# Scores from split fp32r pairs in the attention phase, and the experts' matmuls ahead of the next projection

## What is computed

```python
x = conv(inputs, conv_w) + conv_b             # 3 taps, 1024 -> 3*256, split into q, k, v
qh, kh, vh = (q @ wq + bq), (k @ wk + bk), (v @ wv + bv)   # 16 heads of 64, blocks of 128 tokens
scores = einsum('bqhe,bkhe->bhqk', qh / 8, kh) # causal inside each block of 128
o = softmax(scores) @ vh;  o = o @ wo + bo;  attn = o @ proj_w + proj_b
x = layernorm(x + attn)
base = x @ W_base.T + b_base
w = relu(softmax(x @ W_gate.T) - sigmoid(x @ W_thr.T + b_thr) / 8);  w = w / sum(w)
out = base + 2 * einsum('ner,ne,eor->no', x @ A, w, B)     # 8 experts of rank 16
x = layernorm(x + out)
```

## Time and profile before

| | |
|---|---|
| median of 3 runs | 1757.93 us (1756.76 to 1758.82) |
| the profiled execution | 1758.82 us, span of its instructions 1757.0 us |
| PE busy | 1702.0 us, 97% of the span |
| PEld busy | 1532.1 us, 87% |
| DVE busy | 1298.4 us, 74% |
| ACT busy | 678.1 us, 39% |
| POOL busy | 328.2 us, 19% |
| mean granted TensorE clock | 0.989 |

### The profile page before, as it was taken

One profiled execution on the slowest core, in us unless ns is written; L12 is line 12 of the kernel. 1 busy time (PEld: TensorE's weight loads), 2 busy tenths in 40 slices (PEclk: granted clock), 3 DMA queues, 4 the chain that ended last, 5 costly groups with the idle time before them and its releaser, 6 DMA issues. The chain is left out here.

```text
span 1757.0 us, 32959 instructions
## 1 busy us (share of the span) xinstructions
PE 1702.0 (97%) x11968; PEld 1532.1 (87%) x11968; DVE 1298.4 (74%) x3089; ACT 678.1 (39%) x1817; POOL 328.2 (19%) x272
## 2 busy tenths in 40 slices
PE   6899999999999899999999999989999999999998
PEld 5899999999999778888888888869999898999887
DVE  8977679987677566666666666777787887878785
ACT  4333324332333466766767766761111111111110
POOL 5200003400000100100101002053333333333331
PEclk9999999999999899999999999999999999999999
DMA  4323223332234200110110102141212111121211
GB/s 142 115 80 96 80 82 108 127 114 78 79 95 156 102 1 10 40 48 0 48 48 0 48 22 79 64 137 47 77 54 81 54 68 66 61 73 54 81 39 49
DMA packets 48805, 123.04 MB, mean 70 GB/s; under 512 B 5488, under 2 KB 13680, under 8 KB 48240
## 3 DMA queue, kind: packets, MB, share of 16 engines
q1 hardware_dynamic: 48752, 122.36, 21.2%
HBM read 88.79 MB, written 33.55 MB: 70 GB/s over the span
## 5 line engine op out<-in xcount | busy, mean ns | idle before, releaser
L388 PE MATMUL conv_acc<-x_split,weights 128*128 128x256 f32 x4608 | 557.8, 284 | 30.9 <-DVE weights L314 23.5
L388 PEld LDWEIGHTS conv_acc<-x_split,weights 128*128 128x128 f32 x4608 | 554.8, 191 | 33.6 <-DVE weights L314 25.2
L1315 PE MATMUL ps_f<-weights 128*128 128x266 f32 (+2 forms) x1728 | 329.5, 343 | 0.0
L1315 PEld LDWEIGHTS ps_f<-weights 128*128 128x128 f32 x1728 | 277.4, 189 | 23.9
L247 ACT ACTIVATE x_split<-x_mixed 128x1024 fp32r<-128x1024 f32 x128 | 135.7, 1060 | 308.2 <-PE conv_acc L388 278.7
L309 DVE TENSOR_TENSOR x_split<-x_mixed,x_split 128x1024 fp32r<-128x1024 f32 x128 | 158.7, 1240 | 100.5 <-ACT x_split L247 100.5
L803 DVE CUSTOM_DVE_ANT_0 scores_and_probs<-ps_scores,causal_mask 128x128 f32<-128x128 f32 x512 | 118.6, 287 | 127.6 <-PE ps_scores L923 123.8
L710 ACT ACTIVATE scores_and_probs<-scores_and_probs,score_neg_max 128x128 f32<-128x128 f32 x512 | 197.9, 391 | 4.8 <-DVE score_neg_max L808 4.7
L1151 ACT ACTIVATE gate_exp<-h_and_gate,gate_neg_max 128x8 f32<-128x8 f32 x32 | 9.6, 301 | 348.5 <-DVE gate_neg_max L1226 348.5
L676 POOL TENSOR_TENSOR weights<-conv_tile,weights 128x1024 fp32r<-128x1024 f32 x14 | 35.7, 2551 | 439.1 <-ACT weights L696 353.9
L1315 PE MATMUL ps_f<-late_weights,weights 128*128 128x266 f32 (+2 forms) x576 | 116.1, 337 | 0.0
(11 more groups left out here) (115 smaller groups left out, 2423.1 us busy)
## 6 DMA issues: line engine op xcount, KB each, us to landing
x_raw<-in_xT SPq DMA_DIRECT2D x128, 257.0 KB, 2.7
conv_tile<-in_x SPq DMA_DIRECT2D x32, 512.0 KB, 3.4
out<-out_tile SPq DMA_DIRECT2D x32, 512.0 KB, 2.7
convT_scratch<-features_out SPq DMA_DIRECT2D x16, 768.0 KB, 3.5
conv_tile<-convT_scratch SPq DMA_DIRECT2D x16, 768.0 KB, 6.3
conv_w_raw<-in_conv_w SPq DMA_DIRECT2D x16, 576.0 KB, 4.0
weight_stage<-in_ffn_w SPq DMA_DIRECT2D x8, 581.0 KB, 3.7
yT_scratch<-features_out SPq DMA_DIRECT2D x8, 512.0 KB, 3.7
```

The source lines that it names most:

```text
L388: last = nc.tensor.matmul(acc[f][k // 2][:, k % 2, :], w[:, c, a, k, f * P:(f + 1) * P], xs[:, c % XS, b, k, :], start=(c == 0 and k % 2 = ...
L1315: mm = nc.tensor.matmul(ps_f[par][n][:, 0:b0 - a0], x1T[:, par, a, kc, :], wf[kc][:, b, a0:b0], start=(kc == 0 and k == 0), stop=(n == 2 a ...
```

## The change

**First part (attention).** q and k are stored as fp32r pairs, high and low. ScalarE writes the high parts: q in one instruction, k in two (`k_out`, one for each head of the pair, because each head's k goes to columns of its own). VectorE gets a new step `qk_out` of three instructions that write the low parts, straight from PSUM: two for k (64 partitions each) and one for q. It stands between `normalize` and `mask_max`. `q_ready` and `k_ready` are now raised by VectorE. k has for each block two groups of 128 columns, one for each head: head 0's k in partitions 0 to 63 of the first group, head 1's in partitions 64 to 127 of the second; the other halves are zero, written once by four memsets on GpSimd. So one matmul of 128 x 128 weights (both heads of q) and 256 columns gives the scores of both heads for one block. `make_scores` makes three of them (`PASSES`) for each block, 12 in all, in place of 8 plain fp32 ones. Bank 0 now holds blocks 0 and 1 and bank 1 blocks 2 and 3, and `s_done` is raised after blocks 1 and 3. The two late feed-forward weights lie in the same memory as q and k from the last phase on.

**Second part (feed-forward).** `experts(i)` stands ahead of `project(i + 2)`.

```diff
-        qk = sb("q_and_k", [P, 2, 2, ST], F32)
-        self.k, self.q = qk[:, 0, :, :], qk[:, 1, :, :]
-        late = sb("late_weights", [P, self.LATE * 2 * WCOLS], F32R)
+        k_cols, q_cols = 2 * 2 * BLK * 2 * P, 2 * 2 * ST
+        pair = sb("q_k_pairs", [P, k_cols + q_cols], F32R)
+        self.k = pair[:, 0:k_cols].rearrange("p (i h b j n) -> p i h b j n", i=2, h=2, b=BLK, j=2)
+        self.q = pair[:, k_cols:].rearrange("p (i h n) -> p i h n", i=2, h=2)
...
+            for i in range(2):
+                for j in range(2):
+                    nc.gpsimd.memset(k[rows(1 - j), i, :, :, j, :].bitcast(F32), 0.0).then_inc(k_zeroed, 1)
+            pool.wait_ge(k_zeroed, 4)
...
-                nc.scalar.activation(q[:, s % 2, :], ps_qt[:], ACT.Identity, bias=bq[:, s:s + 1]).then_inc(q_ready, 1)
+                nc.scalar.activation(q[:, s % 2, HI, :], ps_qt[:], ACT.Identity, bias=bq[:, s:s + 1]).then_inc(q_hi, 1)
...
-                nc.scalar.activation(k[:, s % 2, :], ps_kt[:], ACT.Identity, bias=bk[:, s:s + 1]).then_inc(k_ready, 1)
+                for j in range(2):
+                    nc.scalar.activation(k[rows(j), s % 2, HI, :, j, :],
+                                         ps_kt[rows(j), :].rearrange("p (b n) -> p b n", b=BLK), ACT.Identity,
+                                         bias=bk[rows(j), s:s + 1]).then_inc(k_hi, 1)
...
+            def qk_out(g, s):
+                for j in range(2):
+                    dve.wait_ge(k_hi, 2 * g + j + 1)
+                    last = nc.vector.scalar_tensor_tensor(
+                        out=k[rows(j), s % 2, LO, :, j, :], in0=ps_kt[rows(j), :].rearrange("p (b n) -> p b n", b=BLK),
+                        scalar=bk[rows(j), s:s + 1], in1=k[rows(j), s % 2, HI, :, j, :].bitcast(F32),
+                        op0=ALU.add, op1=ALU.subtract)
+                last.then_inc(k_ready, 1)
+                dve.wait_ge(q_hi, g + 1)
+                nc.vector.scalar_tensor_tensor(out=q[:, s % 2, LO, :], in0=ps_qt[:], scalar=bq[:, s:s + 1],
+                                               in1=q[:, s % 2, HI, :].bitcast(F32), op0=ALU.add,
+                                               op1=ALU.subtract).then_inc(q_ready, 1)
...
                     normalize(pair(t, s), s)
+                    if exists(t, s + 2):
+                        qk_out(pair(t, s + 2), (s + 2) % HP)
                     if exists(t, s + 1):
                         mask_max(pair(t, s + 1), s + 1)
...
             v_out(0, 0, slice(0, ST))
+            qk_out(0, 0)
             v_out(1, 1, slice(0, ST))
+            qk_out(1, 1)
...
-                    cols = slice(b * P, (b + 1) * P)
-                    for j in range(2):
-                        last = nc.tensor.matmul(ps_s[j][:, cols], q[rows(j), s % 2, cols], k[rows(j), s % 2, cols],
-                                                start=True, stop=True)
-                        if b == BLK - 1:
-                            last.then_inc(s_done, 1)
+                    for i, (a, c) in enumerate(PASSES):
+                        last = nc.tensor.matmul(ps_s[b // 2][:, b % 2 * 2 * P:(b % 2 + 1) * 2 * P],
+                                                q[:, s % 2, a, b * P:(b + 1) * P], k[:, s % 2, c, b, :, :],
+                                                start=(i == 0), stop=(i == 2))
+                    if b % 2 == 1:
+                        last.then_inc(s_done, 1)
...
-                        last = nc.tensor.transpose(out[:, b * P:(b + 1) * P], probs[:, s % 2, j * BLK + b, :], ident[:])
+                        last = nc.tensor.transpose(out[:, b * P:(b + 1) * P], probs[:, s % 2, 2 * b + j, :], ident[:])
...
             project_qk(1, 1, (k_ready, q_ready), 1)
+            pe.wait_ge(k_zeroed, 4)
             make_scores(0, 0, True)
...
                 base(i, par, 1, range(CC // 2, CC))
+                experts(i, par)
                 if not last(n, 2):
                     project(i + 2, par)
-                experts(i, par)
```

More of the change, by code:

```diff
@@ L445, in __init__ @@
         self.wf = [parts(wq + 2 * WCOLS * k, WCOLS) for k in range(kept)]
-        self.wf += [late[:, 2 * WCOLS * k:2 * WCOLS * (k + 1)].rearrange("p (i n) -> p i n", i=2) for k in range(self.LATE)]
+        self.wf += [pair[:, 2 * WCOLS * k:2 * WCOLS * (k + 1)].rearrange("p (i n) -> p i n", i=2) for k in range(self.LATE)]
         self.wb = parts(attn.start[attn.WO] + 2 * attn.NW, DM)
@@ L585, in attention_phase @@
         v_done, v_ready = sem("v_done"), sem("v_ready")
+        k_zeroed = sem("k_zeroed")
         qk_done = sem("qk_done")
+        q_hi, k_hi = sem("q_hi"), sem("k_hi")
         q_ready, k_ready = sem("q_ready"), sem("k_ready")
```

## The result

The changed kernel takes 1789.5 us (median of 4 runs, 1789.06 to 1792.86); the kernel before took 1757.35 us beside it. The ratio is 1.0186, 95% interval 1.0169 to 1.0204: 32 us slower. The profiled execution took 1788.9 us, its span 1787.1.

A forecast was written before the change was run, and what follows sets the result against it. TensorE, practically without holes, was taken to bound both changed phases. The profiled 1758.8 us plus 20 (attention) and 14 (feed-forward) gave 1792.8, predicted as 1792 because the profiled run lies 0.9 over the median; range 1776 to 1806.

The forecast's parts named there:

- Scores, TensorE: Attention score matmuls: 12 new ones plus a change of form make each step 0.32 us longer, +20 us over 64 groups.
- The cover on VectorE: Attention step: three new 0.69 us instructions fill VectorE's 2.04 us hole and cost nothing; transposes leave 0.9 us.
- Once a tile: Next tile's Q projection waits for GpSimd's split; the split shifts 0.2 us, TensorE 0.32, six times: about -1 us.
- Start and last tile: Memsets at the start cost 0; in the last tile ScalarE also splits feed-forward weights, +1 us.
- The four memsets: GpSimd before the first scores: at most 2.40 us each, 9.6 in all, ending at 601.7 before 602.09; cost 0.
- The ring: Feed-forward window: experts, projection and VectorE's chain back to hT_lo take 18.52 us against TensorE's 18.05; 30 windows, +14 us.
- The two small additions of the prediction: Feed-forward window: 0.05 us for the semaphore and 0.09 until matmuls stream again after a stop.
- A: Feed-forward: the experts' new place costs nothing, so only the attention's +20 remains, 1778 us; chance 0.12.
- B: Attention: VectorE is late with q and k each step, instructions taking 1.26 us; +53 on top, 1845 us; chance 0.08.
- C: Attention: new scores cost less, if the old 8 matmuls run one after the other; -30 us, end 1742; chance 0.04.

The follow-up runs named there:

- experiments 1 and 2: Changed kernel with the old feed-forward order: 1775.67 us. Then kernel before with only experts ahead of project: 1772.62 us.
- experiment 4: Changed kernel with 552 unused columns behind the q and k pairs, so later tensors lie in their old places: 1794.93 us, ratio 1.0208.
- Experiments 6 and 7: Changed kernel with extra q-low-part VectorE instructions each step (two: 1847.14 us; one: 1803.63 us); then changed kernel with 4 score matmuls, not 12: 1761.67 us.
- Experiment 5: Changed kernel with VectorE's split of hT moved ahead of its split of the next block's x1T: 1774.79 us, ratio 1.0094.
- experiment 2: Kernel before with only the feed-forward order changed, experts ahead of project: 1772.62 us, ratio 1.0076.
- experiment 8: Kernel before with the score loop over heads outside, all blocks of head 0 and then of head 1: 1787.92 us, ratio 1.0168.

## Why the prediction was right, and where it was off

Predicted 1792, measured 1789.5; attention +20 and feed-forward +14 predicted, +17.3 and +14.2 measured (experiments 1 and 2). Both mechanisms came about as described: more work on a full TensorE in the attention phase, a ring through VectorE in the feed-forward part. That the number lies within 2.5 us is in part luck. The layout made the kernel 4 to 6 us faster, which the sum did not have, and both terms of the sum were a little low (0.32 us a step taken, 0.35 measured; 0.47 us a window taken, 0.51 to 0.55 measured). With the old places (experiment 4) the time is 36.6 us over the kernel before, where 34 were predicted.

- **Scores, TensorE.** Predicted +0.32 us a step. With equal places it is +0.35 (experiment 4 against before). 12 matmuls step every 0.119 us, and the change of form behind them costs 0.09, where 0.118 and 0.08 were taken. This term was right.
- **The places of the tensors.** Not in the prediction at all: -4.4 to -5.4 us in the changed kernel, -5.9 in the kernel before. It is why a step grew by 0.27 only. Left out, they are more than the whole distance from 1792 to the measured time.
- **The cover on VectorE.** Right in direction and nearly in size: the k and q instructions take 0.75 us, not 0.69, q's low part has 0.69 us to spare (858.94 - 858.25), not 0.9. Experiments 6 and 7 show both sides of that limit. That the transposes do not wait holds for the usual step; in the last tile they do, three times, by 1.24, 0.14 and 0.64 us.
- **Once a tile.** TensorE's longer step there was 9.10 against 8.68 and is 9.33 against 8.95: 0.04 less, 6 times, so -0.2 us and not -1.
- **Start and last tile.** Two early steps take 8.26 and 9.06 us where they took 7.38 and 8.64, which is 0.8 us more than twice 0.27 (0 taken); the last seven take 3.3 us more in all, 1.5 more than seven times 0.27 (+1 taken). The four memsets took 3.8 us and lie in GpSimd's idle time, as said. But the 2.40 us taken as the dearest row for them was not that: the earlier trace rows have one of 4.50, by which they would have ended after the first scores.
- **The ring.** Predicted 18.52 us, measured 18.56 in the middle of the loop. It closes with the rows after: 0.05 (1503.87 to 1503.92), 1.61 for the experts with their restart, 3.01 to VectorE's second half (1508.54 - 1505.53), and 13.89 for its chain (1489.98 to 1503.87). The two small additions of the prediction, 0.05 and 0.09, had no row beside them; they measure 0.05 and 0.10. TensorE waits 29 times, not 30, and the first and last few windows are shorter, 18.4 us. Experiment 5 shows the mechanism: cut the chain by one place, and the window is TensorE's again.
- **Rivals.** A (the reorder costs nothing) fell with experiment 2. B (VectorE late) did not come about, but is closer than 0.08 suggested: one more instruction costs 14 us. C fell with experiment 8: the heads did run side by side, so its condition was false. Its price was not tested: in experiment 8's 1.64 us three records still run beside others. Sixteen records one after the other at 0.112 us would be 1.79, an estimate near the 1.89 of its count.

## What to carry to other kernels

Where one engine has no hole, its cost per group of instructions, read as the distance between starts, gave the price of this edit within a few hundredths of a microsecond. The busy shares did not show the stall: VectorE was busy for 14.5 us of a window of 18.05 and its chain, waits included, still became the limit. Before two groups are exchanged on the full engine, close the ring: sum the other engine's chain and the groups that stand between its end and its start, and compare with the loop's period; slack of 4 us vanished here for a move of 2.8 us and a delay of 1.5. And before giving credit or blame for a few microseconds to an edit that also changes the size of a buffer, run the old code with the new layout.

## What the runs showed that was not expected

The place of one tensor in memory changes TensorE's pace. With `heads_out` 552 columns (2208 bytes a partition) lower, the 512-column matmuls of the output, K and Q projections start every 0.227 us with little scatter (half of the distances are 0.226 to 0.227); in the old place every 0.224 to 0.238. In the kernel before, the V projection moves the other way (median 0.233 against 0.231), with the place of `scores_and_probs` or what lies around it; in the changed kernel it is 0.232 with either places.

Only the output projection reads `heads_out`. The kernel before has one early step with no output projection ahead of K:

```profile
628.79 1.52 PE L909 MATMUL ps_k_and_probsT<-weights 128*128 128x512 f32 x6
...
629.60 0.68 DVE L825 TENSOR_TENSOR heads_out<-ps_heads_out,heads_out 128x512 fp32r<-128x512 f32 x1
630.15 1.52 PE L909 MATMUL ps_q_and_probsT<-weights 128*128 128x512 f32 x6
```

There K takes 630.15 - 628.79 = 1.36 us in the old place, while VectorE writes `heads_out`. So in this one step K is at the faster pace without the output projection ahead of it, and that write does not slow it. Why K and Q keep its pace is open, and so is which other access meets the reads. No other distances than 552 columns were tried, so no rule for good places follows.
